# Group-norm sums of a retention layer moved from VectorE reductions to ScalarE accumulating activations

## The reference, cut to what matters

```python
x = x + attn(layernorm(x))          # retention with decay, 8 heads, value width 256 a head
x = x + ffn(layernorm(x))           # one of 8 experts is chosen for the whole sequence
# inside attn:
ret = out.transpose(0, 2, 1, 3).reshape(b, t, V_DIM)            # V_DIM = 2048
g = ret.reshape(b * t, N_HEADS, V_DIM // N_HEADS)               # 256 values a head
mu = g.mean(-1, keepdims=True)
var = ((g - mu) ** 2).mean(-1, keepdims=True)
normed = ((g - mu) * jax.lax.rsqrt(var + GN_EPS)).reshape(b, t, V_DIM)
gate = jax.nn.silu(hidden_states @ W_g)
proj_out = gate * normed @ W_proj
```

## Time and profile before

| | us |
|---|---|
| median of 3 runs | 3274.38 |
| lowest and highest of these | 3267.69 and 3337.62 |
| the profiled execution, as timed | 3271.48 |
| its span, slowest core (core 2) | 3269.8 |
| busy: TensorE / VectorE / ScalarE | 1670.4 / 1276.1 / 589.8 |

### The profile page before, as it was taken

The page is one execution under the profiler, slowest core; times in us unless marked ns, Lnnn a source line. Parts: engine busy times, 40 slices in busy tenths (PEclk is TensorE's granted clock), DMA queues, the critical chain, the costliest instruction groups (busy, mean ns, idle before and its releaser), DMA issues.

```text
span 3269.8 us, 28847 instructions; the slowest of 8 cores (3239.1 to 3269.8 us)
## 1 busy us (share of the span) xinstructions
PE 1670.4 (51%) x8174; PEld 847.4 (26%) x8174; DVE 1276.1 (39%) x2357; ACT 589.8 (18%) x1132; POOL 137.6 (4%) x208
## 2 busy tenths in 40 slices
PE   0065655555646555565555564655555555643133
PEld 0022322223222323232222322232322223232121
DVE  1015244252525252533526253525335262525433
ACT  0012221221112121222112221211221111211000
POOL 0100000000000000000000000000000000000100
PEclk6577777776868778677777686777777686866555
DMA  7873442434353525334244435343342434332475
GB/s 130 111 216 111 133 164 91 160 109 167 129 174 129 174 93 160 127 119 158 88 163 135 167 129 174 110 148 122 110 162 89 167 129 147 129 122 74 139 246 211
DMA packets 156946, 459.24 MB, mean 140 GB/s; under 512 B 14197, under 2 KB 26486, under 8 KB 146294
## 3 DMA queue, kind: packets, MB, share of 16 engines
q1 hardware_dynamic: 128694, 344.13, 31.5%
q0 software_dynamic: 18880, 46.14, 7.3%
q10 hardware_dynamic: 9216, 67.11, 5.2%
HBM read 432.17 MB, written 58.72 MB: 150 GB/s over the span
## 4 chain that ended last, share of the span: by engine, by line
PE 35%; DVE 24%; DMA 15%; ACT 13%; issue 10%; POOL 2%; DVEq 1%; ACTq 1%; SPq 0%; POOLq 0%
DMA wp<-wproj_bf 6%; PE PA L568 6%; DMA wqkvg_bf<-wqkvg 4%; PE PA L502 4%; PE PB L502 3%; PE PC L378 3%; PE PA L755 3%; PE PB L755 3%; PE PC L568 3%; ACT v_sb L578 2%; DMA outT<-out_sb 2%; PE PD L568 2%; DVE gst L693 2%; DVE gst L690 2%; POOL xp_sb L769 2%
## 5 line engine op out<-in xcount | busy, mean ns | idle before, releaser
L568 PE MATMUL PA<-wnb,lnx_sb 128*128 128x512 bf16 x1024 | 337.4, 414 | 49.3 <-ACT v_sb L578 27.6
L568 PE MATMUL PC<-wnb,lnx_sb 128*128 128x512 bf16 x512 | 213.9, 418 | 238.6 <-ACT v_sb L578 213.4
L755 PE MATMUL PA<-ggT_sb,wp 128*128 128x256 bf16 x1024 | 239.0, 322 | 137.0 <-DMA wp<-wproj_bf 109.3
L367 DVE TENSOR_TENSOR ao_sb<-qs_sb 128x1024 bf16<-128x1024 bf16 x64 | 44.3, 692 | 574.1 <-ACT qs_sb L364 574.1
L502 PE MATMUL PA<-wnb,lnx_sb 128*128 128x512 bf16 x512 | 172.8, 422 | 166.4 <-DMA wnb<-wqkvg_bf 151.2
L755 PE MATMUL PB<-ggT_sb,wp 128*128 128x256 bf16 x1024 | 239.6, 323 | 23.9 <-ACT pe_sc L766 23.9
L568 PE MATMUL PD<-wnb,lnx_sb 128*128 128x512 bf16 x512 | 211.4, 413 | 14.9 <-ACT v_sb L578 6.7
L378 PE MATMUL PC<-qs_sb,ones_bf 128*1 128x256 bf16 x256 | 59.7, 412 | 279.9 <-ACT qs_sb L364 279.9
L502 PE MATMUL PB<-wnb,lnx_sb 128*128 128x512 bf16 x512 | 168.3, 413 | 3.3 <-ACT qbf L513 3.3
L755 PEld LDWEIGHTS PA<-ggT_sb,wp 128*128 128x128 bf16 x1024 | 106.2, 113 | 201.7 <-issue 176.0
L568 PEld LDWEIGHTS PA<-wnb,lnx_sb 128*128 128x128 bf16 x1024 | 101.8, 104 | 198.7 <-issue 107.7
(11 more groups left out here) (215 smaller groups left out, 2692.1 us busy)
## 6 DMA issues: line engine op xcount, KB each, us to landing
wnb<-wqkvg_bf SPq DMA_DIRECT2D x384, 512.0 KB, 5.3
wp<-wproj_bf SPq DMA_DIRECT2D x256, 512.0 KB, 6.4
x<-xt ACTq DMA_DIRECT2D x16, 1024.0 KB, 4.6
tab<-tabs ACTq DMA_DIRECT2D x16, 1024.0 KB, 6.7
xp<-xp_sb ACTq DMA_DIRECT2D x16, 1024.0 KB, 7.8
x<-xp POOLq DMA_DIRECT2D x16, 1024.0 KB, 9.3
outT<-out_sb ACTq DMA_DIRECT2D x16, 1024.0 KB, 4.9
wqkvg_bf<-wqkvg POOLq DMA_DIRECT2D x12, 1024.0 KB, 9.4
```

Source lines behind the costliest of these rows:

```text
L367: S.op("vector", lambda E, a=a, b=b: E.tensor_tensor(xsq_fl[:, a:b], xbf_fl[:, a:b], xbf_fl[:, a:b], ALU.mult), reads=[xbf_fl[:, a:b]], wr ...
L568: S.op("tensor", lambda E, m=m, k=k, P=P, wb=wb: E.matmul(P, lnx_sb[:, k, m * 128:(m + 1) * 128], wb[:, k % 4, :], start=(k == 0), stop=(k ...
L755: S.op("tensor", lambda E, vtp=vtp, sub=sub, vt=vt, f=f, P=P, fo=fo: E.matmul(P[:, fo:fo + C], wp_sb[vtp % 4][:, sub, f * 128:(f + 1) * 12 ...
```

## The change

`gn_phase` no longer squares and reduces on VectorE. In place of L687, L690 and L693, ScalarE runs 32 activations a chunk over `ao_sb`, one Copy and one Square for each of the 16 pieces of 256 columns. Each also gives out the sum of its results along the row (`accum_out`) into one column of `gst`; the elementwise results go to the scratch tile `sc_sb` and are not used. From L696 on everything stays.

```diff
     def gn_phase(c):
-        aof = ao_sb[:].rearrange("p i n -> p (i n)")
-        S.op("vector", lambda E, aof=aof: E.tensor_tensor(
-            gg_sb[:].rearrange("p i n -> p (i n)"), aof, aof, ALU.mult),
-            reads=[ao_sb[:]], writes=[gg_sb[:]])
-        S.op("vector", lambda E: E.tensor_reduce(
-            gst[:, 0:16], ao_sb[:].rearrange("p i (h n) -> p (i h) n", n=256),
-            AX.X, ALU.add), reads=[ao_sb[:]], writes=[gst[:, 0:16]])
-        S.op("vector", lambda E: E.tensor_reduce(
-            gst[:, 16:32], gg_sb[:].rearrange("p i (h n) -> p (i h) n", n=256),
-            AX.X, ALU.add), reads=[gg_sb[:]], writes=[gst[:, 16:32]])
+        for i in range(MT):
+            for h in range(HH):
+                col = i * 8 + h
+                seg = ao_sb[:, i, h * 256:(h + 1) * 256]
+                S.op("scalar", lambda E, seg=seg, col=col: E.activation(
+                    sc_sb[:, 0:256], seg, AF.Copy, accum_out=gst[:, col:col + 1]),
+                    reads=[seg], writes=[sc_sb[:, 0:256], gst[:, col:col + 1]])
+                S.op("scalar", lambda E, seg=seg, col=col: E.activation(
+                    sc_sb[:, 0:256], seg, AF.Square, accum_out=gst[:, 16 + col:17 + col]),
+                    reads=[seg], writes=[sc_sb[:, 0:256], gst[:, 16 + col:17 + col]])
```

## The result

The changed kernel took 3315.0 us (median of 9 runs) and the kernel before 3288.9 us in the 10 runs beside which it was judged; the ratio is 1.0132, with a 95% interval from 1.0102 to 1.0161. Measured again later, on the chip of the last experiments, it was 1.0098 (1.0071 to 1.0125). The forecast was +33 us, a ratio of 1.010. The change makes the kernel about 1% slower, which is less than the 2% of the prediction's line between "same" and "slower". In some executions of either kernel the cores of a die show a lower granted clock and the time is longer (3384 us for the changed one, its cores down to 0.67), and the ratio is formed from the others alone, so that it isn't the quotient of the two medians, 1.008. Of the times, only ratios are compared from here on: the median of the kernel before was 3274.4 us in its first three runs and 3288.9 in ten.

The account below looks back on a forecast made before the run. No engine's work bounds it; TensorE stalls for the v copy behind the statistics in ScalarE's queue. Sums delay L696 by 2.2 us, +33 us in 15 chunks, +0.1 in the last: 3274.4 + 33 = 3307 us, range 3261 to 3374.

Parts of the forecast that it names:

- The place: ScalarE's queue: v copy L578 stands behind Ln and the statistics, so L696's start sets TensorE's 13.8 us stall.
- The link: Start-to-start pitch of the 32 chained ScalarE activations with their accumulator reads: 0.60 us each.
- a read that doesn't overlap: Accumulator read starts only after its activation ends: 0.73 us a link, +100 us, 3374 us; chance 0.28.
- a free read: Accumulator read adds nothing to the activation chain: 0.51 us a link, -13 us, 3261 us; chance 0.12.
- The start: First activation starts without a wait, 0.09 us before the k copy ends, 5.8 us ahead of VectorE's old start.
- The sum: 32 sums take 19.1 us; L696 starts 2.2 us later, +33 us in 15 chunks, +0.1 us in the last.
- The rest: Profile signs: VectorE busy down 178 us, its L696 wait some 13 us a chunk, Ln wait 1.5, table loads 33.
- the third rival: Square needs another ScalarE table, loads before first Square and Ln: 41 us added, 3348 us; chance 0.02.
- The rule on simple arithmetic: Skill rule favouring VectorE, up to three times faster: sums 33 us a chunk, over 200 us slower; prediction rejected it.
- the cover: Margin between VectorE's last scaling pair ending at 1585.49 and the gate copy at 1589.93: 4.4 us, expected to stay.
- the fourth rival: VectorE's relief counts: over 2% faster, needing 0.40 us a link before L696; called nearly excluded.

Follow-up runs that it names:

- the kernel with v first: Kernel before with the first v pair (product and copies) emitted ahead of gn_phase(c), changing only ScalarE's order: ratio 0.9888 to the kernel before.

## Why the prediction was right

- *The place.* The prediction said that ScalarE's queue, not its load, decides: the v copy stands behind Ln, and Ln behind the sums. The ten runs agree with it. The stall for the v copy and the time go together in both directions: 105, 148, 202, 213, 247 and 308 us of wait give 0.969, 0.979, 0.995, 1, 1.010 to 1.013, and 1.035.
- *The link.* Forecast 0.60 us from 0.41 - 0.09 + 0.18 + 0.10. Measured: 416 ns, overlap 0.09, read 186 ns, gap 0.09, and 0.60 between starts. Each part was read off another instruction of the kernel before, and each held. That the read overlaps its activation was taken from the k copies by analogy, with a chance of 0.55, so on this point the forecast was also fortunate; the rival of a read that doesn't overlap (0.73) and that of a free read (0.51) are both out.
- *The start.* The first activation begins 0.11 us before the k copy ends (forecast 0.09), with no wait.
- *The sum.* Forecast 2.2 us of longer stall a chunk, 33 us; the wait grew by 33.3. In the chunk shown it is 2.5, since one link of the chain has a pause of 0.37 us instead of 0.09; nothing in the profile names its cause. Ten of the 15 chunks have the 2.2 us exactly. The last chunk, where +0.1 us was forecast, isn't in this wait: there L696 starts 19.31 us after ScalarE's last copy of `ao_sb` (3007.18 - 2987.87), where it was 19.23 before. The profiled execution grew by 37.1 us, so 4 us are not explained, 0.1%.
- *The rest.* VectorE's busy time fell by 175 us (178 forecast), its wait ahead of L696 is 13.3 us a chunk (13 forecast), and Ln waits 1.50 us. ScalarE's table loads stay 33: Square needed no load of its own beside Ln and Exp, and the third rival is out.
- *The rule on simple arithmetic.* The prediction weighed the rule of the Trainium skill ("ScalarE: Activation LUTs", "Rules for kernel authors") that such work belongs on VectorE, and estimated 33 us a chunk by it. Measured, the chain takes 19.4 us in the chunk shown. The direction of the rule holds here all the same: 32 activations of 0.416 us are 13.3 us for two passes over 4096 columns, the reads not counted, where VectorE took 11.1 for three. The prediction argued against it with the time of one more column (0.83 ns against 1.08); with the fixed part, which it named right after, an activation takes 416 / 256 = 1.6 ns a column. What the change cost was then set by where the work stood.
- *Two readings that were off and did no harm.* The last reader of the gate is L722, not L727 of the earlier trace rows, and what waits is the table load: the cover was 1588.63 - 1584.90 = 3.7 us, not 4.4. And 0.40 us a link is no impossible figure, as the fourth rival has it ("less than one activation alone"): with two sets of tensors the links came to just that.
- *What was not seen.* The prediction asked what the change costs at its place. It passed by the larger thing that stands in the timeline of the same chunk of the kernel before: just ahead, ScalarE waits 16.2 us for the q product and VectorE 9.4 us for ScalarE's copy of it, and nearly all of the statistics fit in there.

```profile
1539.11 1.02 ACT L513 ACTIVATE qbf<-PA 128x1024 bf16<-128x1024 f32 x1 [16.20 <-PE PA L502]
1540.31 0.42 DVE L538 TENSOR_TENSOR rt<-qbf,tab 128x512 bf16<-128x512 bf16 x1 [9.39 <-ACT qbf L513]
```

## What to carry to other kernels

An engine that is 18% busy can still have no room at one place: ask what stands behind the new work in that engine's queue and who waits for it, and price the work by its pitch there, gaps and reads included. Where one copy that frees PSUM stands in a queue behind work that it doesn't need, moving that work into an earlier idle stretch took 4.5 to 7% off the time here, where giving it to ScalarE at its old place added 1% (or took off 2%, with the links untied) and sharing it between the two engines took off 3%. In a chain of short instructions, alternate the output tensors, so that none waits for its direct predecessor.

## What the runs showed of the hardware

- An accumulator read on ScalarE takes 186 ns but adds only 0.09 us to the pitch of chained activations, since it starts before its activation ends.
- The wait of an activation for the last one's read cost 0.20 us a link (0.60 against 0.40 us between starts), twice the gap of 0.10 us that the timeline shows, because the overlap with the predecessor goes too.
- An activation of 256 columns takes 416 ns on 128 partitions and 415 on one.
- In the kernel with v first ScalarE's table load was not done during the 14.03 us of waiting ahead of it: it started only when VectorE's last pair had released the gate, and its 1.28 us stood between the release and the gate copy.
